# A graph kernel's normalization stage: a static table of pairs instead of rounds, with six batches summed on GpSimd without relu

## What is computed

```python
h = jnp.maximum(_layernorm(x, axis=-1), 0.0)          # per batch and row, over 1024
x_avg = h.mean(over the 64 batches)                   # 1024 nodes x 128
x_norm = x_avg / norm(x_avg)
sim = (x_norm @ x_norm.T + 1.0) * 0.5                 # 1024 x 1024
A = (sim + gumbel0 > 1 - sim + gumbel1)               # edges
Wn = normalized(A, common neighbours)                 # 1024 x 1024
out = x + Wn.T @ (h @ weight) + bias                  # per batch
```

## Time and profile before

| what | value |
|---|---|
| median of 3 runs | 954.95 us (954.63 to 955.58) |
| the profiled execution | 955.32 us |
| its span, first to last instruction | 953.6 us |
| busy, whole span | PE 908.6, PEld 771.2, DVE 725.9, ACT 352.3, POOL 213.6 us |
| stage 1 | from 0 to about 117 us; similarity products start at 125.44 us |

### The profile page before, as it was taken

The page is one execution under the profiler, slowest core; times in us unless marked ns, Lnnn a source line. Parts: engine busy times, 40 slices in busy tenths (PEclk is TensorE's granted clock), DMA queues, the critical chain, the costliest instruction groups (busy, mean ns, idle before and its releaser), DMA issues.

```text
span 953.6 us, 12576 instructions
## 1 busy us (share of the span) xinstructions
PE 908.6 (95%) x4615; PEld 771.2 (81%) x4619; DVE 725.9 (76%) x1499; ACT 352.3 (37%) x565; POOL 213.6 (22%) x178
## 2 busy tenths in 40 slices
PE   2988899888999999999999999999999999999997
PEld 0655565777888888888898888888988888888886
DVE  7789678899978879785767675858676766767587
ACT  3999817431212121223333334242424242424130
POOL 2677733002211111120111111111111111111111
PEclk9999999999999999999999999999999999999999
DMA  9999981301707244342433424152424242424022
GB/s 357 351 350 343 393 328 61 134 23 44 252 30 249 81 184 147 118 168 98 135 131 110 156 92 175 66 192 74 177 89 177 89 176 89 177 68 175 29 105 89
DMA packets 36587, 149.75 MB, mean 157 GB/s; under 512 B 2864, under 2 KB 2992, under 8 KB 33456
## 3 DMA queue, kind: packets, MB, share of 16 engines
q1 hardware_dynamic: 36528, 148.97, 42.8%
HBM read 107.02 MB, written 41.94 MB: 156 GB/s over the span
## 4 chain that ended last, share of the span: by engine, by line
PE 83%; DVE 8%; ACT 4%; issue 2%; DMA 1%; SPq 0%; ACTq 0%; DVEq 0%
PE ps L1346 67%; PE ps L1286 7%; ACT main L496 3%; DVE bmem L945 3%; PE ps L1120 2%; PE ps L1141 2%; PE ps L1208 2%; PE ps L1189 1%; DVE bmem L938 1%; DVE stats L732 1%; DMA main<-in_x 1%; ACT bmem L522 0%; DVE main L1056 0%; DVE bmem L957 0%; PE ps L1265 0%
## 5 line engine op out<-in xcount | busy, mean ns | idle before, releaser
L1346 PE MATMUL ps<-bmem,main 128*128 128x256 f32 x3136 | 692.5, 380 | 3.0 <-DVE main L1023 2.6
L1346 PEld LDWEIGHTS ps<-bmem,main 128*128 128x128 f32 x3136 | 590.7, 190 | 80.8 <-DVE main L1023 3.0
L466 POOL TENSOR_TENSOR main<-main 128x256 f32<-128x256 f32 x32 | 25.2, 788 | 541.6 <-ACT main L633 482.8
L1023 DVE TENSOR_TENSOR main<-ps,main 128x512 f32<-128x512 f32 x124 | 76.4, 622 | 83.9 <-PE ps L1346 83.9
L604 ACT ACTIVATE main<-ps 128x512 f32<-128x512 f32 x88 | 52.5, 597 | 210.9 <-PE ps L1286 210.9
L1032 DVE TENSOR_TENSOR main<-main 128x256 f32<-128x256 f32 (+1 forms) x256 | 119.3, 536 | 0.0
L456 POOL TENSOR_TENSOR main<-main 128x256 f32<-128x256 f32 (+1 forms) x96 | 92.0, 986 | 119.1 <-DVE main L1016 119.1
L1286 PEld LDWEIGHTS ps<-w_sb,main 128*128 128x128 f32 x704 | 92.4, 192 | 9.0 <-issue 2.8
L1286 PE MATMUL ps<-w_sb,main 128*128 128x128 f32 x704 | 93.5, 276 | 3.9 <-ACT main L604 3.9
L1141 PE MATMUL ps<-main,ident 128*128 128x512 f32 x128 | 63.2, 628 | 26.6 <-ACT main L496 26.6
L863 DVE TENSOR_TENSOR main<-main 128x256 f32<-128x256 f32 x112 | 46.9, 419 | 54.5 <-PE ps L1346 51.2
(11 more groups left out here) (98 smaller groups left out, 534.5 us busy)
## 6 DMA issues: line engine op xcount, KB each, us to landing
main<-in_x SPq DMA_DIRECT2D x61, 1024.0 KB, 6.7
out<-main SPq DMA_DIRECT2D x31, 1024.0 KB, 4.9
main<-in_x SPq DMA_DIRECT2D x50, 512.0 KB, 5.7
bmem<-in_L_gnn_gumbel SPq DMA_DIRECT2D x8, 1024.0 KB, 8.0
spill<-bmem SPq DMA_DIRECT2D x8, 1024.0 KB, 14.5
main<-spill SPq DMA_DIRECT2D x8, 1024.0 KB, 6.9
out<-main SPq DMA_DIRECT2D x1, 512.0 KB, 4.9
out<-main SPq DMA_DIRECT2D x2, 256.0 KB, 4.6
```

What stands on the lines that cost most here:

```text
L1023: dve.tensor_tensor(at, piece(slot, b), at, ALU.add).then_inc(s, 1)
L1346: last = pe.matmul(piece(slot, b)[:, QUARTER * e:QUARTER * (e + 1)], left_[:, blk(c)], right_[:, c, :], start=slot in FRESH and b < 3 and ...
```

## The change

Stage 1's loops go; all five engines run through the 32 pairs written out, by a table of groups. The first and the last pair are groups of their own, the others go by two: [0], [1, 2], [3, 4], ..., [29, 30], [31]. The chain of a group is done at once for the first three groups and the last two. The pairs in `SPILLED` and `AHEAD` change places accordingly (the number of kept products stays 16). For the six pairs in `POOLED` (6, 10, 14, 18, 22, 26) ScalarE makes no relu of the even batch. GpSimd makes max(x * rstd, mean * rstd) in place in `xin`, which is the relu plus mean * rstd, and adds that; VectorE computes each pair's mean * rstd (`floor`), and subtracts their sum when it adds the two partial sums. A pooled pair's slot of `xin` is free only when GpSimd's add is done. Batch 62, the last even one, is summed by TensorE, and late product 0 stands behind that sum.

```diff
-    SPILLED = [0, 2] + list(range(GROUP, PAIRS - GROUP, GROUP))
-    AHEAD = [1, 3]
+    SPILLED = [1, 3, *range(5, PAIRS - 3, 4)]
+    AHEAD = [0, 2]
+    KEPT = 2 * len(SPILLED)
+    GROUPS = [[0], *([p, p + 1] for p in range(1, PAIRS - 1, 2)), [PAIRS - 1]]
+    GROUP_OF = {p: t for t, pairs in enumerate(GROUPS) for p in pairs}
+    POOLED = [p for p in range(4, PAIRS - 2) if p % 4 == 2]
...
                     sp.wait_ge(s_h, 2 * (p - XPAIRS) + 2)
+                    if p - XPAIRS in POOLED:
+                        sp.wait_ge(s_even, p - XPAIRS + 1)
...
+            for p in range(PAIRS - 1):
+                if p in POOLED:
+                    n = 2 * p
+                    at = xin[:, p % XPAIRS, 0, :]
+                    pool.wait_ge(s_row, GROUP_OF[p] + 1)
+                    j = POOLED.index(p)
+                    pool.tensor_scalar(at, at, rstd[:, n:n + 1], floor[:, j:j + 1], ALU.mult, ALU.max
+                                       ).then_inc(s_norm, 1)
+                    pool.wait_ge(s_norm, j + 1)
+                    wait(pool, s_even, p)
+                    pool.tensor_tensor(hsum[:, :], hsum[:, :], at, ALU.add).then_inc(s_even, 1)
+                else:
...
+            def relu(p):
+                act.wait_ge(s_row, GROUP_OF[p] + 1)
+                wait(act, s_even, p - HPAIRS + 1)
+                wait(act, s_odd, p - HPAIRS + 1)
+                for b in range(1 if p in POOLED else 0, 2):
...
+            std(0)
+            for t, pairs in enumerate(GROUPS):
+                for p in pairs:
+                    if t == 0 or t == len(GROUPS) - 1:
+                        relu(p)
+                        if t == 0:
+                            std(1)
+                    elif p == pairs[0] and t > 1:
+                        relu(p)
+                        std(t + 1)
+                    elif t == 1:
+                        relu(p)
+                        if p == pairs[1]:
+                            std(2)
...
+                    if p - HPAIRS + 1 in SPILLED:
+                        keep(p - HPAIRS + 1)
...
+                for p in GROUPS[t]:
+                    if p in POOLED:
+                        j, b = POOLED.index(p), 2 * (p - GROUPS[t][0])
+                        dve.scalar_tensor_tensor(out=floor[:, j:j + 1], in0=mean[:, b:b + 1], scalar=1.0,
+                                                 in1=again[:, b:b + 1], op0=ALU.mult, op1=ALU.mult).then_inc(s_floor, 1)
...
+            for t, pairs in enumerate(GROUPS):
+                steps = 4 * len(pairs)
+                if t < 3:
+                    for c in range(steps):
+                        last = long_step(t, c)
+                    last.then_inc(s_bn, 1)
+                    aggregate(t)
+                    whole_chain(t)
+                elif t == len(GROUPS) - 1:
+                    aggregate(t - 1)
+                    long_step(t, 0)
+                    whole_chain(t - 1)
+                    for c in range(1, steps):
+                        last = long_step(t, c)
+                    last.then_inc(s_bn, 1)
+                    aggregate(t)
+                    whole_chain(t)
+                else:
+                    long_step(t, 0)
+                    long_step(t, 1)
+                    for c, between in enumerate((aggregate, invert, quotient, newton, set_rstd, set_shift), 1):
+                        if t > 3:
+                            between(t - 1)
+                        last = long_step(t, c + 1)
+                    last.then_inc(s_bn, 1)
...
-                dve.tensor_tensor(hsum[:, half(f)], ps[:, f, :], hsum[:, half(f)], ALU.add).then_inc(s_sum, 1)
+                dve.scalar_tensor_tensor(out=hsum[:, half(f)], in0=ps[:, f, :], scalar=dmax[:, 0:1],
+                                         in1=hsum[:, half(f)], op0=ALU.subtract, op1=ALU.add).then_inc(s_sum, 1)
...
+            for p in range(PAIRS):
+                pe.wait_ge(s_h, 2 * p + 2)
+                for b in ((0, 1) if p == PAIRS - 1 else (1,)):
                     for f in range(2):
...
+                if p in SPILLED:
+                    keep_product(p, 0)
+                if p - 1 in SPILLED:
+                    keep_product(p - 1, 1)
+
+            pe.wait_ge(s_kept, KEPT)
+            late_times_weight(0, 2)
```

More of the change, by code:

```diff
@@ L428, in _ @@
             pool.tensor_copy(identh[:, :], ident[:, :]).then_inc(s_const, 1)
[L431 to L438, removed]
+            for p in range(PAIRS - 1):
[10 more added lines that the diff above has]
+                else:
+                    pool.wait_ge(s_h, 2 * p + 1)
+                    wait(pool, s_even, p)
+                    pool.tensor_tensor(hsum[:, :], hsum[:, :], h1[:, p % HPAIRS, 0, :], ALU.add).then_inc(s_even, 1)
             pool.wait_ge(s_unit, 2)
@@ L482, in _, with std @@
             act.activation(dmax[:, 3:4], eps_sb[:, :], ACT.Sqrt)
-            def std(g, turn, b0=0, b1=4):
-                act.wait_ge(s_mv, turn + 1)
-                act.activation(half_std[:, g % 2, b0:b1], mv[:, g % 2, b0:b1, 1], ACT.Sqrt, bias=eps_sb[:, :],
+            def std(t):
+                n = 2 * len(GROUPS[t])
+                act.wait_ge(s_mv, t + 1)
+                act.activation(half_std[:, t % 2, 0:n], mv[:, t % 2, 0:n, 1], ACT.Sqrt, bias=eps_sb[:, :],
                                scale=0.25).then_inc(s_std, 1)
[L489 to L507, removed]
-                    else:
[L509 to L528, removed]
@@ new lines, in keep @@
+            def keep(p):
+                for b in range(2):
+                    n = 2 * SPILLED.index(p) + b
+                    act.wait_ge(s_hw, n + 1)
+                    act.activation(kept[:, n, :], bank(2 + 2 * b, 2), ACT.Copy).then_inc(s_kept, 1)
+            std(0)
[12 more added lines that the diff above has]
+                            std(2)
+                    else:
+                        relu(p)
+                    if p - HPAIRS + 1 in SPILLED:
+                        keep(p - HPAIRS + 1)
@@ L662, in _, with rows @@
             dve.wait_ge(s_const, 5)
[L668 to L674, removed]
+            def rows(t):
+                g, n = t % 2, 2 * len(GROUPS[t])
+                return (half_std[:, g, 0:n], *(small[:, g, c, 0:n] for c in range(3)), mv[:, g, 0:n, 0], mv[:, g, 0:n, 1])
@@ L675, in aggregate, with batches, invert @@
+            def batches(t):
+                return slice(2 * GROUPS[t][0], 2 * GROUPS[t][-1] + 2)
+            def aggregate(t):
+                dve.wait_ge(s_bn, t + 1)
+                for b in range(2 * len(GROUPS[t])):
+                    last = dve.bn_aggr(mv[:, t % 2, b, :], stats[:, t % 2, b, :])
                 last.then_inc(s_mv, 1)
-            def invert(g, turn, b0=0, b1=4):
-                half, _, _, inv, *_ = rows(g, b0, b1)
-                dve.wait_ge(s_std, turn + 1)
+            def invert(t):
+                half, _, _, inv, *_ = rows(t)
+                dve.wait_ge(s_std, t + 1)
@@ L718, in first @@
[L718 to L743, removed]
-                                whole_chain(g, four, 0, 2)
-                            elif end and g == FOURS - 1 and c == 3:
-                                long_step(c).then_inc(s_bn, 1)
-                            else:
-                                long_step(c)
-                    else:
-                        long_step(0)
-                        if before:
-                            dve.wait_ge(s_bn, four)
-                        long_step(1)
-                        if before:
-                            aggregate(g - 1)
-                        long_step(2)
-                        if before:
-                            invert(g - 1, four - 1)
-                        long_step(3)
-                        if before:
-                            quotient(g - 1, four - 1)
-                        long_step(4)
-                        if before:
-                            newton(g - 1, four - 1)
-                        long_step(5)
-                        if before:
-                            set_rstd(g - 1, four - 1)
-                        long_step(6)
-                        if before:
-                            set_shift(g - 1, four - 1)
-                    long_step(7).then_inc(s_bn, 1)
@@ new lines, in whole_chain, with long_step @@
+            def whole_chain(t):
+                invert(t)
+                quotient(t)
+                newton(t)
+                set_rstd(t)
+                set_shift(t)
+            def long_step(t, c):
+                p, b, f = GROUPS[t][c // 4], c // 2 % 2, c % 2
+                if f == 0 and p < SINGLE:
+                    dve.wait_ge(s_x[p] if b else s_x_first[p], 16)
+                elif f == b == 0:
+                    dve.wait_ge(s_x[p % XPAIRS], (p // XPAIRS + 1) * 16)
+                return dve.bn_stats(stats[:, t % 2, c // 2, 6 * f:6 * f + 6], xin[:, p % XPAIRS, b, half(f)])
@@ L1126, in late_times_weight, with keep_product @@
```

(17 more changed lines are left out.)

90 lines of the change are left out of this document (28 added, 62 removed).

## The result

The changed kernel takes 962.11 us (median of 4, 960.96 to 962.37), the kernel before 954.79 us beside it: ratio 1.0075, interval 1.0059 to 1.0091, 7.3 us slower. The forecast was no measurable change, 956.4 us, with a range up to 959.5. The column sums start at 126.17 us instead of 119.84, so 6.3 of the 6.7 us that the span grew (953.6 to 960.3) arise in stage 1.

The account below looks back on a forecast made before the run. Stage 1's rhythm decides when stage 2 starts: VectorE's shifts make the short step, ScalarE's keeps the long one. Column sums -0.1 and half-speed TensorE product +1.6 give +1.5 us, 956.4 us; range 951.5 to 959.5.

Parts of the forecast that it names:

- The rhythm of 5.50 and 6.53 us and its two causes: Stage 1 std-to-std steps: VectorE's shifts make the short one, ScalarE's two keeps the long one; 12.03 us for four pairs.
- the start: First relus in stage 1: relu 0 starts at 8.5, relu 1 at 15.45, relu 3 at 22.4.
- the hole from 24.4 to 28.25: ScalarE idle from 24.7 to 29.0 before group 3's std, losing most of the 3.6 us early start.
- TensorE's half-speed product at 31.77: Product 3 after TensorE's 2.4 to 4 us pause takes 3.38 instead of 1.78; relu 7 starts 1.6 us later.
- the 7.3 us at the end: TensorE's sums and late products before the column sums now run from relu 31's end, giving back 2.4 us.
- I take 1.6, between memset (no input) and add (two inputs): GpSimd's multiply-and-max on a pooled pair takes 1.6 us, so GpSimd needs 11.4 us in four pairs, under 12.03.
- The point of decision, 2.27 us: Time of GpSimd's multiply-and-max from which GpSimd becomes the bound: 12.03 less 9.76 us for four pairs.
- rival C: GpSimd becomes the bound: at 3.15 us for the new operation, 2.9 us more, 959.3; chance 0.12.
- the ring and the cover: In rival C, the ring of four h1 slots and the final 3 us cover absorb some 2.4 us of GpSimd's lateness.
- B: Saved relus count because ScalarE's sum holds the rhythm: 0.88 us in each of six cycles, 951.1; chance 0.20.
- A: TensorE's clock holds at 32 us, so the 1.6 us fall away: 954.9; chance 0.20.
- the loads of pooled slots are hidden with 2 us in hand: SyncE loads waiting for GpSimd's add: pair 14's is issued at 40.5, lands at 45.6, is needed at 48.

Follow-up runs that it names:

- the early keep: Against the change with no pair pooled: ScalarE copies pair 1's product ahead of group 3's std instead of behind relu 4; 954.8 us, ratio 0.9997.
- the run with the old end: Against the change with no pair pooled: GpSimd adds the last even batch, late product 0 ahead of pair 31's sum; 955.4 us, ratio 1.0001.
- the kernel with pairs 8, 16, 24: The change with three pooled pairs (8, 16, 24) instead of six, all in the step with ScalarE's keeps; 955.87 us, ratio 1.0002.
- the profiles at 955.15 and 956.99: Profiled runs of two variants of the change: multiply-and-max left out (median 959.34 us), and the multiply alone, without the floor (median 958.56 us).

## Why the prediction was wrong, point by point

**What held.** The rhythm of 5.50 and 6.53 us and its two causes; that the pooled pairs of the change lie in the step that VectorE holds and so gain nothing (three of them in that place: 957.26 against 957.11), except for pair 6, which lies in a step with keeps; the start, the hole from 24.4 to 28.25, TensorE's half-speed product at 31.77 with the keep behind it (forecast 1.6 for the half speed; the early keep, which takes away the pause too, gave 2.3); the 7.3 us at the end, now from relu 31 (1.7 us by the run with the old end, forecast 2.4). The forecast without GpSimd's term, 956.4, lies 0.7 us under the kernel with none pooled (957.11). With the pooled batches added raw it is less clear: 955.15 in one run, and 958.87 to 959.79 in four.

**What failed** is one term, in the part on the change: "I take 1.6, between memset (no input) and add (two inputs)". It is 3.78 us. By it GpSimd needs 13.7 us in four pairs and not 11.4, sets the pace instead of keeping under it, and its lateness reaches the relus over the slots of `xin` and VectorE's final sum over the last add. The row had been chosen by the number of inputs, and the count of operations is what costs: 1.05 for a copy, 2.8 with one operation, 3.6 to 3.8 with two. The upper end of the bounds, 3.15 for an add that was held up, lay below the truth as well, since I ordered the operation below an add by its inputs and no row excluded the contrary. The point of decision, 2.27 us, is borne out as far as the runs go: with 2.84 us for the operation GpSimd already runs without pauses and is a little late, with nothing it is not; no run lies closer. The rival C that stands on it is what happened. It had a chance of 0.12 and a price from 3.15. With 3.78 the working of that rival gives 4 x 2.44 + 3.78 = 13.5 in four pairs, 1.5 over the rhythm, 9.1 us in six, 6.7 after the 2.4 that the ring and the cover take: 963.1 against 962.11. So close a hit is part luck, since the 2.4 was a rough figure and no run measures it. The GPSIMD Engine Reference in the Trainium skill (section 3.1) has 1.03 cycles per element for such a body, 0.88 us by the estimate in the prediction; the trace disagrees by a factor of more than four, and the measurement decides. I let it weigh for the low end of a term that no row showed.

**The other rivals.** B needs the saved relus to count; they would in the other place (1 us each, by the steps of the kernel with pairs 8, 16, 24), not in that of the change. A, the clock held through the pause, did not come in the profiled run of the change, whose pause was 3.13 us; it was seen in the profiles at 955.15 and 956.99, with pauses of 2.08 and 2.10 us. The signs that were named for being wrong came: the operation above 2.3 us, GpSimd without pauses, VectorE waiting for x. The statement that the loads of pooled slots are hidden with 2 us in hand held for pair 14 and failed for pair 22, because GpSimd's lateness adds up from round to round.

## What to carry to other kernels

Before work is moved off an engine, find the step in which that engine sets the pace: here three relus saved in one half of the period were worth nothing, two of three saved in the other half shortened their steps by 1 us each, and moving one keep of each product across was worth 3.1 us. An operation that no trace shows should be bounded by what it computes as well as by what it reads; where the engine that receives it has a known point of decision, a run of that one operation is worth more than any estimate. And a short stall of TensorE on a copy that ScalarE makes later than it could can be paid twice: here the pause was 3.13 us, and the sixteen matmuls behind it took 3.68 us, where the same product at full clock took 1.95.

## What the runs showed of the hardware

GpSimd on 128x1024 f32: copy 1.05 us, multiply 2.77 (constant) or 2.85 (column), multiply and max 3.63 to 3.78, add of two tensors 2.39. TensorE's granted clock after a pause did not follow from the length of the pause alone: in stage 2 the same sixteen matmuls stand behind a pause of 2.34 or 2.35 us in the kernel before, the change and the kernel with raw adds, and they ran at a granted clock of 0.57 in the kernel before (3.38 us), 0.55 in the change (3.52 us) and 1.00 with raw adds (2.05 us). Differences of 1 to 2 us between medians can hold such a share, so the readings above rest on steps and waits in the traces beside the medians.
